# Reordering the first two tiles and projecting queries and keys as three products of parts, in a pre-norm retention and mixture-of-experts block

## The reference

```python
# attention with decay, chunk by chunk; S is the state that is carried on
h = layernorm(x)
q, k, v = h @ Wq, h @ Wk, h @ Wv            # split into heads
attn    = (qc @ kc.T) * D                   # within a chunk, D a table of decays
o       = attn @ vc + (qc * decay_q) @ S
S       = decay_s * S + (kc * decay_k).T @ vc
x       = x + concat(o) @ Wo
# experts
h       = layernorm(x)
probs   = softmax(h @ Wg); w, i = top_k(probs, 2); w = w / (sum(w) + 1e-8)
y[e]    = square(relu(h @ W1[e])) @ W2[e]   # all tokens, every expert
x       = x + sum_e combine[:, e] * y[e]
```

## Time and profile before

| | |
|---|---|
| time, median of 3 executions | 295.58 us (295.46 to 301.28) |
| profiled execution | 295.8 us, its span 292.9 us |
| busy: PE, DVE, POOL, ACT | 277.2, 219.7, 190.9, 176.4 us |
| mean granted clock of TensorE | 0.987 of full speed |
| moved by transfers | 26.79 MB, mean 91 GB/s |

### The profile page before, as it was taken

The page is one execution under the profiler, slowest core; times in us unless marked ns, Lnnn a source line. Parts: engine busy times, 40 slices in busy tenths (PEclk is TensorE's granted clock), DMA queues, the critical chain, the costliest instruction groups (busy, mean ns, idle before and its releaser), DMA issues.

```text
span 292.9 us, 8869 instructions
## 1 busy us (share of the span) xinstructions
PE 277.2 (95%) x3650; PEld 216.9 (74%) x3650; DVE 219.7 (75%) x569; ACT 176.4 (60%) x253; POOL 190.9 (65%) x152
## 2 busy tenths in 40 slices
PE   7977886999999999999999999999999998999995
PEld 5665465778787778877787777877787787888883
DVE  3746967796569967697569966699569858898883
ACT  2622629646675559746585549756585466686961
POOL 1113595977487786787487785787587874465752
PEclk9997799999999999999999999999999999999999
DMA  7119273004240240604241040304230051305301
GB/s 228 44 24 332 81 248 117 3 0 147 76 135 11 67 157 2 181 0 147 75 121 61 8 186 31 110 2 143 79 102 9 6 165 54 110 8 210 107 0 72
DMA packets 13704, 26.79 MB, mean 91 GB/s; under 512 B 1120, under 2 KB 6752, under 8 KB 13664
## 3 DMA queue, kind: packets, MB, share of 16 engines
q1 hardware_dynamic: 13664, 26.23, 28.0%
HBM read 24.00 MB, written 2.23 MB: 90 GB/s over the span
## 4 chain that ended last, share of the span: by engine, by line
POOL 36%; PE 28%; issue 24%; ACT 5%; DVE 3%; DMA 2%; POOLq 1%; DVEq 0%; ACTq 0%
POOL act_lo L1113 34%; PE h_ps L371 3%; POOL rstd L1085 2%; PE h_ps L373 2%; PE h_ps L372 2%; PE y_ps L398 2%; PE y_ps L392 2%; DMA scale<-w 2%; PE y_ps L393 2%; PE bank L511 1%; PE bank L522 1%; PE bank L432 1%; ACT act_sf L1008 1%; PE h_ps L415 1%; PE y_ps L347 1%
## 5 line engine op out<-in xcount | busy, mean ns | idle before, releaser
L1113 POOL TENSOR_TENSOR act_lo<-act_sf,act_hi 128x512 fp32r<-128x512 f32 x112 | 150.6, 1366 | 54.9 <-ACT act_sf L1008 54.6
L815 DVE SCALAR_TENSOR_TENSOR act_sf<-h_ps,scale 128x1024 f32<-128x1024 f32 x64 | 77.9, 1219 | 47.4 <-PE h_ps L373 21.1
L1001 ACT ACTIVATE act_hi<-act_sf 128x1024 fp32r<-128x1024 f32 x64 | 68.1, 1064 | 56.4 <-DVE act_sf L815 56.3
L1008 ACT ACTIVATE act_sf<-act_sf 128x1024 f32<-128x1024 f32 x64 | 67.3, 1052 | 0.0
L371 PE MATMUL h_ps<-x_hi,w_lo 128*128 128x512 f32 x128 | 54.9, 429 | 0.9 <-ACT act_sf L969 0.9
L373 PE MATMUL h_ps<-x_hi,w_hi 128*128 128x512 f32 x128 | 50.5, 394 | 0.0
L372 PE MATMUL h_ps<-x_lo,w_hi 128*128 128x512 f32 x128 | 50.4, 394 | 0.0
L392 PE MATMUL y_ps<-act_hi,w_lo 128*128 128x512 f32 x112 | 47.0, 420 | 0.0
L393 PE MATMUL y_ps<-act_hi,w_hi 128*128 128x512 f32 x112 | 44.0, 392 | 0.0
L398 PE MATMUL y_ps<-act_lo,w_hi 128*128 128x512 f32 x112 | 35.2, 396 | 0.1
L1085 POOL TENSOR_TENSOR rstd<-variance,minus_half 128x4 f32<-128x4 f32 x16 | 16.1, 1008 | 23.9 <-DVE variance L660 23.8
(11 more groups left out here) (143 smaller groups left out, 424.7 us busy)
## 6 DMA issues: line engine op xcount, KB each, us to landing
scale<-scratch SPq DMA_DIRECT2D x32, 512.0 KB, 4.1
x_t_in<-x_tr SPq DMA_DIRECT2D x8, 256.0 KB, 5.0
x_all<-x SPq DMA_DIRECT2D x8, 256.0 KB, 5.1
out<-out_sb SPq DMA_DIRECT2D x8, 256.0 KB, 4.3
scale<-w SPq DMA_DIRECT2D x1, 1024.0 KB, 5.4
cst<-constants SPq DMA_DIRECT2D x1, 288.0 KB, 4.7
cst<-constants SPq DMA_DIRECT2D x1, 256.0 KB, 2.7
cst<-constants SPq DMA_DIRECT2D x1, 232.0 KB, 5.0
```

Source lines behind the costliest of these rows:

```text
L815: nc.vector.scalar_tensor_tensor(out=act_s[:, u % 2], in0=h_ps[:, u % 2], scalar=0.0, in1=scale[:, f % 2, e].unsqueeze(1).to_broadcast([P, ...
L1001: nc.scalar.activation(act_hi[:, u % 4], act_s[:, u % 2], ACT.Square).then_inc(act_hi_ready, 1)
L1008: nc.scalar.activation(act_f[:, u % 2], act_s[:, u % 2], ACT.Square).then_inc(act_f_ready, 1)
L1113: nc.gpsimd.tensor_tensor(act_lo[:, u % 4, n], act_f[:, u % 2, n], act_hi[:, u % 4, n].bitcast(F32), ALU.subtract).then_inc(pool_low_ready, 1)
```

## The change

It has two parts.

The first reorders tiles 0 and 1. The first two experts of W1 are loaded by a transfer of their own right behind load(1), and only the other six wait for tile 0's outputs. On PE, tile 0's outputs and tile 1's scores come ahead of tile 1's values and transposed keys, and the first expert product w1_product(0, 0) ahead of tile 1's outputs. For this tile 1's scores and its updates and outputs get other banks (score_bank and chunk_bank). DVE, ACT and POOL are reordered to match: tile 1's decay_scores come around add_attention(0), scan_states(1) behind spread_roots(0), high_second ahead of copy_roots(0), low_second ahead of the last two low pieces, and in the first turn of the loop keep_x(1) ahead of the second square, and on PE transpose_x2 in slot 0, transpose_k in slot 4, route in slot 6. The waits are set anew.

The second part holds for tiles 3 to 7. The projections of queries and keys, each a float32 matmul of 128x512, become three float32r products: of the weights' low part by the high part of x, high by low, high by high. The high parts are casts on ACT (high_qk once, high_input per tile), the low parts subtractions on POOL (low_qk, low_input), made one turn of the loop ahead. The values are still projected in float32.

```diff
 LENT = 5
+SPLIT_FROM = 3
...
         w_center = sb("w_center", [P, 3, P])
+        qk_hi, qk_lo = (sb(n, [P, 2, P], F32R) for n in ("qk_hi", "qk_lo"))
+        xt_hi, xt_lo = (sb(n, [P, 2, TILE], F32R) for n in ("xt_hi", "xt_lo"))
...
             if s == 1:
-                return (b1[1], b2[1], b0[1], b0[0])[pair]
+                return (center_bank[0], center_bank[1], b2[1], b0[0])[pair]
...
         def chunk_bank(s, c):
-            return (b1, b2)[c][buffers(s)]
+            return (b2[0], b0[0])[c] if s == 1 else (b1[0], b2[0])[c]
         def router_bank(s):
...
         center_loaded, w_center_done, w_center_ready = sem("center_loaded"), sem("w_center_done"), sem("w_center_ready")
-        w1_loaded, w2_loaded = sem("w1_loaded"), sem("w2_loaded")
+        w1_pair_loaded, w1_loaded, w2_loaded = sem("w1_pair_loaded"), sem("w1_loaded"), sem("w2_loaded")
...
         w2_high, w2_low = sem("w2_high"), sem("w2_low")
+        qk_hi_ready, qk_lo_ready = sem("qk_hi_ready"), sem("qk_lo_ready")
+        xt_hi_ready, xt_lo_ready = sem("xt_hi_ready"), sem("xt_lo_ready")
...
             load(1)
+            sp.dma_start(w1_in[:, 0:2], w1[0:2].rearrange("e d h -> d e h")).then_inc(w1_pair_loaded, DMA)
...
-            sp.dma_start(w1_in, w1.rearrange("e d h -> d e h")).then_inc(w1_loaded, DMA)
+            sp.dma_start(w1_in[:, 2:EXPERTS], w1[2:EXPERTS].rearrange("e d h -> d e h")).then_inc(w1_loaded, DMA)
...
                     pe.wait_ge(x_lo_ready, 1)
-                    pe.wait_ge(o_t_ready, 2)
+                    pe.wait_ge(k_d_ready, 2)
+                    pe.wait_ge(v_z_ready, 2)
...
-                    pe.wait_ge(piece_whole, PIECES)
+                    pe.wait_ge(attn_ready, PAIRS + 3)
+                    pe.wait_ge(piece_whole, 4)
...
                 if u == 0:
-                    pe.wait_ge(root_t_ready, 1)
+                    pe.wait_ge(piece_whole, PIECES)
...
                 elif i == 1:
+                    pe.wait_ge(w1_pair_loaded, DMA)
+                elif i == 2:
...
-                if i >= 2:
+                if i < 2:
+                    pe.wait_ge(attn_ready, PAIRS + i + 1)
+                else:
...
+                if i == 4:
+                    pe.wait_ge(root_t_ready, 1)
...
                           start=True, stop=True).then_inc(piece_done, 1)
+            def split_product(to, which, s):
+                pe.matmul(to, qk_lo[:, which], xt_hi[:, s % 2], start=True, stop=False)
+                pe.matmul(to, qk_hi[:, which], xt_lo[:, s % 2], start=False, stop=False)
+                return pe.matmul(to, qk_hi[:, which], xt_hi[:, s % 2], start=False, stop=True)
             def project_q(s):
...
                 pe.wait_ge(x_t_loaded[s % XT_RING], DMA * (s // XT_RING + 1))
-                if before(s):
-                    pe.wait_ge(o_t_ready, before(s))
+                if s >= 2:
+                    pe.wait_ge(o_t_ready, s)
...
                     pe.wait_ge(root_t_ready, s - 1)
-                pe.matmul(b2[b], w_center[:, 0], x_t_in[:, s % XT_RING], start=True, stop=True).then_inc(q_done, 1)
+                if s >= SPLIT_FROM:
+                    pe.wait_ge(qk_lo_ready, 1)
+                    pe.wait_ge(xt_lo_ready, s - SPLIT_FROM + 1)
+                    split_product(b2[b], 0, s).then_inc(q_done, 1)
+                else:
+                    pe.matmul(b2[b], w_center[:, 0], x_t_in[:, s % XT_RING], start=True, stop=True).then_inc(q_done, 1)
             def project_k(s):
...
                     pe.wait_ge(attn_ready, 1)
-                pe.matmul(b0[b], w_center[:, 1], x_t_in[:, s % XT_RING], start=True, stop=True).then_inc(k_done, 1)
+                if s >= SPLIT_FROM:
+                    split_product(b0[b], 1, s).then_inc(k_done, 1)
+                else:
+                    pe.matmul(b0[b], w_center[:, 1], x_t_in[:, s % XT_RING], start=True, stop=True).then_inc(k_done, 1)
             def project_v(s):
...
             def scores(s):
...
                 pe.wait_ge(q_m_ready, s + 1)
-                if s >= 1:
+                if s == 1:
+                    pe.wait_ge(attn_ready, PAIRS)
+                    pe.wait_ge(k_d_ready, 1)
+                    pe.wait_ge(q_d_ready, 2)
+                    pe.wait_ge(k_t_ready, 2)
+                elif s >= 2:
...
                     pe.wait_ge(q_d_ready, s + 1)
-                if s >= 2:
...
             def state_updates(s):
                 b = buffers(s)
+                if s <= 1:
+                    pe.wait_ge(k_d_ready, s + 1)
+                    pe.wait_ge(v_z_ready, s + 1)
...
-                    pe.wait_ge(k_d_ready, 1)
-                    pe.wait_ge(v_z_ready, 1)
...
+                elif s == 1:
+                    pe.wait_ge(o_t_ready, 1)
+                    pe.wait_ge(logit_sum_ready, 1)
+                    pe.wait_ge(attn_ready, PAIRS * 2)
...
-                    pe.wait_ge(attn_ready, PAIRS * s + (2 if s == 1 else 3))
+                    pe.wait_ge(attn_ready, PAIRS * s + 3)
...
             def transpose_roots(s):
...
                 if s == 0:
-                    pe.wait_ge(piece_whole, PIECES)
+                    pe.wait_ge(piece_whole, 3)
...
                         project_out(p)
-                    if n == 2:
+                    if n == (2 if f >= 1 else 0):
...
-                    if n == (5 if a < TILES else 4):
+                    if n == (6 if f == 0 else 5 if a < TILES else 4):
...
                         project_k(a)
-                    if n == 3:
+                    if n == (3 if f >= 1 else 4):
...
             project_k(1)
+            outputs_within(0)
+            outputs_before(0)
+            scores(1)
+            project_out(0)
...
             transpose_k(1)
-            outputs_within(0)
-            outputs_before(0)
...
-            project_out(0)
-            scores(1)
...
             state_updates(1)
+            w1_product(0, 0)
+            outputs_within(1)
...
-            center_piece(4)
...
-            outputs_within(1)
...
-            w1_product(0, 0)
...
             w1_product(0, 1)
+            center_piece(4)
...
             scan_states(0)
+            decay_q(1)
...
-            decay_q(1)
-            decay_k(1)
+            decay_scores(1, (0, 1))
...
             statistics(0, 1)
+            decay_scores(1, (2,))
...
-            decay_scores(1, (0,))
+            decay_k(1)
+            decay_scores(1, (3,))
...
-            decay_scores(1, (1,))
+            mask_updates(1)
...
-            decay_scores(1, (2, 3))
...
-            mask_updates(1)
...
                 nc.scalar.copy(w2_hi[:], w2_in).then_inc(w2_high, 1)
+            def high_qk():
+                nc.scalar.copy(qk_hi[:], w_center[:, 0:2]).then_inc(qk_hi_ready, 1)
+            def high_input(s):
+                act.wait_ge(x_t_loaded[s % XT_RING], DMA * (s // XT_RING + 1))
+                if s >= SPLIT_FROM + 2:
+                    act.wait_ge(k_done, s - 1)
+                nc.scalar.copy(xt_hi[:, s % 2], x_t_in[:, s % XT_RING]).then_inc(xt_hi_ready, 1)
             def mask_q(s):
...
             high_piece(2)
+            high_second()
+            copy_roots(0)
...
+            copy_o(1)
...
-            copy_roots(0)
-            high_second()
-            copy_o(1)
...
                 a, p, u = f + AHEAD + 1, f + AHEAD, EXPERTS * f
+                if f == 0:
+                    high_x(p)
...
                 if f == 0:
-                    high_x(p)
...
                 square(u)
+                if f == 0:
+                    keep_x(p)
...
                 square(u + 1)
-                if p < TILES:
+                if f >= 1 and p < TILES:
...
                 square(u + 4)
+                if f == 0:
+                    act.wait_ge(w_center_ready, 1)
+                    high_qk()
+                if SPLIT_FROM <= a + 1 < TILES:
+                    high_input(a + 1)
...
                 nc.gpsimd.tensor_tensor(lo, whole, hi.bitcast(F32), ALU.subtract).then_inc(piece_low, 1)
+            def low_qk():
+                pool.wait_ge(qk_hi_ready, 1)
+                nc.gpsimd.tensor_tensor(qk_lo[:], w_center[:, 0:2], qk_hi[:].bitcast(F32), ALU.subtract
+                                        ).then_inc(qk_lo_ready, 1)
+            def low_input(s):
+                pool.wait_ge(xt_hi_ready, s - SPLIT_FROM + 1)
+                if s >= SPLIT_FROM + 2:
+                    pool.wait_ge(k_done, s - 1)
+                nc.gpsimd.tensor_tensor(xt_lo[:, s % 2], x_t_in[:, s % XT_RING], xt_hi[:, s % 2].bitcast(F32), ALU.subtract
+                                        ).then_inc(xt_lo_ready, 1)
             def low_second():
...
             low_piece(2)
+            low_second()
...
             low_piece(4)
-            low_second()
...
                 low(u + 5)
+                if f == 0:
+                    low_qk()
+                if SPLIT_FROM <= a + 1 < TILES:
+                    low_input(a + 1)
...
```

## The result

The changed kernel takes **290.66 us** in the median of four executions (290.6 to 291.6), the kernel before beside it 295.52; the ratio is 0.985, its 95% interval 0.981 to 0.989. So it is 1.5% faster. The forecast was 292.1, the range 288.5 to 294.2. The profiled execution took 291.6 us with a span of 289.8.

What follows compares the result with a forecast made beforehand. TensorE was taken as the bound from the third tile on, with waits before. Early order 5.0, less 3.1 for a clock fall, plus 1.6 for split projections, gave 3.5 us off 295.6: 292.1 us, range 288.5 to 294.2.

Steps and rivals of the forecast that it cites:

- Tile 0's outputs earlier: Before the loop, tile 0's outputs start near 18.7 us, against 19.8; PE's unexplained halt stays, ending near 18.4.
- add_attention(0) at 20.24: Before the loop on DVE: tile 1's scores eat the earlier gain, so add_attention(0) starts at 21.3, against 21.79.
- Weight pair: Before tile 0's router: no wait for the weight transfer (1.64 us before); router at 25.3, PE idling some 1.5 us.
- combine_r came at 31.36: Tile 1 before the loop: combine_r at 32.9, scan done at 34.3, outputs ending at 35.6; PE idles some 2.4 us.
- Third expert's product: After tile 2's projections, PE starts the third expert's product at 41.7, against 46.51; scale_h(0) at 40.2.
- The step that was mis-sized: Tile 2's state updates: two ACT waits go, DVE's choice and masks add 3.3 us; 56.4 against 61.45.
- the early order: Reordering tiles 0 and 1 up to tile 2's state updates: worth 5.0 us when the clock stays up.
- The clock term: PE's clock falls again at about 36 us, in dense work: 3.1 us lost, range 0 to 4.9.
- a fall elsewhere: Sign that the prediction is wrong: the clock's fall not starting near 36 us, where about 6.8 us was expected.
- Split: Query and key projections of tiles 3 to 7 in parts: 0.32 us saved per tile, 1.6 us in all.
- The subtraction was covered: POOL's new subtraction, some 1.3 us per tile, fits idle time before the root, with 0.15 to 0.25 us to spare.
- the slower rival: In the loop, POOL's subtraction is not covered and delays PE by up to 1.37 us per turn: 299.6 at worst, chance 0.04.

Runs made afterwards that it cites:

- the two repeats: The changed kernel unaltered, run again twice beside the kernel before: 292.14 us, ratio 0.9887, and 292.60 us, ratio 0.991.
- the late pair: Changed kernel with the first two experts' weights again fetched only after tile 0's outputs: 293.33 us, ratio 0.9935 to the kernel before.
- small pad: Changed kernel with 16 unused PE products on zeros, 8 columns each, ahead of tile 0's router: 289.76 us, ratio 0.982 to the kernel before.
- the split alone: Kernel before with only the split query and key projections of tiles 3 to 7: 295.63 us, the kernel before 294.23, no ratio.
- the two orders: Changed kernel, first loop turn: POOL's root ahead of low pieces, DVE's second and third score masks ahead of the choice: 293.09 us, ratio 0.994 to before.
- the first pad: Changed kernel with 16 unused PE products on zeros, 64 columns each, ahead of tile 0's router: 292.94 us, ratio 0.989 to the kernel before.

## Why the prediction came out right, point by point

The sign, the size and the verdict "within 2%" were right, with 290.66 for 292.1. The medians fell by 4.9 us for 3.5 forecast, and by 3.7 and 2.4 us in the two repeats. Two terms were off in opposite directions.

1. Tile 0's outputs earlier: the halt at 17.55 to 19.21 was carried along as said, ending at 17.52 (18.4 forecast; 18.06 and 18.07 in the two repeats, whose first projection starts 0.6 later, as before's did).
2. add_attention(0) at 20.24, forecast 21.3; 20.79 in a repeat. Counted from the first projection it is right to half a microsecond.
3. Weight pair: no wait for the transfer, the router behind x_lo at 24.18 with 1.24 us idle (25.3 and 1.5 forecast). But the late pair also met no wait, only some 1 us in all. So the early issue was not what removed the wait. The reader stands later now and the pair is a smaller transfer than the eight experts of before; which of the two did it was not separated.
4. combine_r came at 31.36 (32.9 forecast) and the scan took 0.75 us, not 1.42, and ended at 32.2 (34.3). PE's 2.4 us of idle time ahead of the roots and the scan did not come either; the halt stood in their place. The outputs of tile 1 ended at 36.0, forecast 35.6, because of what I had not forecast, the halt of 2.19 us in their first half. In the repeat with a halt of 0.67 they ended at 35.0.
5. Third expert's product at 42.31 (41.36 in the repeat), forecast 41.7, 46.51 before. scale_h(0) at 40.94, forecast 40.2.
6. **The step that was mis-sized.** State_updates(2) was to run at 56.4 with the clock up. In the one profile with the clock up (small pad) the head is 51.4 us, 50.2 by the forecast: the early order is worth 3.8 us, not 5.0. The term that was wrong is "DVE's choice and two masks take some 3.3 us more". From the exponential to state_updates(2) it is 5.8 us in the first profile, in both repeats and with the small pad, for DVE first has an expert scaling (1.21) and a score mask (0.67), and one operation of 4 columns in the choice takes 1.11 us. Against these 2.5 us the exponential itself came 1.3 sooner than forecast with the clock up (45.6 us after the first projection, 46.9 forecast). The wait of 1.00 us for POOL's root is not the cause: without it the head was as long (51.4). With two masks ahead of the choice it was 48.4, which shows that DVE's order sets this place.
7. **The clock term** was the worst. I took 3.1 us for a fall of 6.8 near 36, and had named a fall elsewhere as a sign of being wrong. It fell at 31.6 in one profile, at 26.3 and 26.4 in the repeats, each time for 3.4 us. With the fall the head is 51.2 to 51.5 us in the repeats and without it 51.4, so the profiles show no cost of it there. But the one profile without a fall also had the slow transfer of the roots to the scratch (3.50 us, 1.4 in the repeats), so what the head would be with neither is open. In the first profile, where halt and fall sit together at 29.3 to 35, the head is 1.5 us longer. Over a whole execution a lower clock went with a longer time: of the changed kernel's ten executions beside the small pad, the two with a mean granted clock of 0.994 had spans of 288.6 and 289.8 us, the five with 0.988 290.7 to 292.6; the turn of state_updates(4), with its halt, is 34.8 us without a fall and 36.2 to 36.5 with one. The head in the first profile is thus 2.3 us shorter than before, 3.7 to 4.0 in the repeats, against 1.9 in my sum.
8. Split: the chain gives 72.05 to 73.43, 1.38 us for 1.71, and five turns sum to 163.3 us without the halt of 2.06, to 165.0 before without its two of 0.41: 1.7 us for 1.6 (1.3 in the profile of the split alone). The six-product price was right.
9. POOL: the root follows the subtraction with 0.26 us of idle time, forecast 0.15 to 0.25. The subtraction was covered, nothing on PE waited for it, and the slower rival did not occur. The turn is full of PE, 32.80 of 32.8 us.

What the sum left out altogether is the halt in a later turn: 2.06 us where before had 0.41 and 0.41. It takes back 1.2 us of the split in this profile. In the repeats, with a fall behind it, that turn is 3.6 to 4.0 us longer than the turns without a halt, 2.8 to 3.2 more than the two short halts of before took. And 1.1 us of the difference between the two profiled executions lie outside the spans: 2.9 us before, 1.8 after. I had taken it as unchanged. In 68 later executions of the kernel before it was 1.9 us in the median and 2.5 or more in 12, so that part of the first profile's gain is mostly the one execution.

So the prediction came close partly by luck: an early order worth less than forecast met a clock term of 0 to 1.5 us where 3.1 were taken off, and a start 0.6 us earlier and the 1.1 us outside the span more than made up for the halt that the sum did not have.

## What to carry to other kernels

Ask of each microsecond taken from PE which engine sets the next meeting point: here three engines stood within 2 us of each other, and removing a halt, a fall of the clock or a wait moved the wait elsewhere (heads of 51.2 to 51.5 us in four profiles with different halts and falls). A change of order in front of a fixed-length loop should be read in the turns behind it too, since a shift in the count of instructions ahead of them changes what lies at the places of the halts. Two edits that each shorten a part need not help together: the pad and the two orders were 0.982 and 0.994 of the kernel before, and together 1.002.

## What the runs showed of the hardware that was not expected

- PE's halts that nothing releases stand at entries 705, 1217, 1473, 2241, 4033, 5057, 5825 and 6849 of its program, each 193 above a multiple of 256, in kernels with different work there. Two rows show how far the program was at the first halt, for the kernel after and the one with the small pad (matmuls and weight loads in brackets):

```profile
0.00:16.29 16.29, 13.98 (x349) 10.15 (x350) 10.19 (x32) 6.64 (x13) 2.23 (x8) 1.00 0.45 139
```

```profile
0.00:16.69 16.69, 14.39 (x349) 10.25 (x350) 10.19 (x32) 6.64 (x13) 2.23 (x8) 1.00 0.44 136
```

They last from 0.4 to 2.4 us or do not show, and are seen only in runs of many products of 32 and 64 columns or within a few entries behind one. A long run is not enough: with the first pad entry 2241 has some 240 such entries ahead of it and no halt, with the small pad the same and a halt of 1.92 us. The profile's instruction queue moves 29 packets, 0.48 MB, some 16 KB each; in the profile after one of them is under way at 29.27, as the halt of 29.32 begins. That the halts are waits for these fetches fits the packets and the count, and the halt at 1217 goes when the large loads are held back; the fetch itself was not changed, so it is argued, not shown.
- A fall of the clock lasted 3.4 us in most profiles, 6.8 in the one of before, 10.2 once. Ahead of most falls PE was busy 1.0 to 2.2 of 3.2 to 3.4 us. But 2.16 of 3.4 us were followed by a fall in a repeat (at 26.4) and by none in the first profile (22.50 to 25.90), and with the first pad, of 1.97 us on zeros, the clock fell at 30.89 behind a stretch in which PE's records leave no gap. So the rows don't tell when it falls.

```profile
27.50:30.90 3.40, 3.40 (x62) 2.55 (x64) 2.37 (x7) 1.17 (x3) 1.73 (x2) 1.00 1.12 311
```

- The scan took 0.75 us ahead of the loop and 1.38 in the median, the long ones beside work on POOL; some DVE operations of 4 to 64 columns took 1.1 to 1.3 us beside POOL's subtractions instead of 0.15 to 0.25. That agrees with the port pair that the Trainium skill (SBUF — State Buffer, section "Who interferes with whom") describes, and by the rows it accounts for about 1 of the 2.5 us in point 6 (the operation of 4 columns, 1.11 us, which took 0.15 before).
